# Four weight copies ahead of the semaphore clears, and block tables read sixteen at a time

## The reference

```python
# L0_ffn: 8 experts, hidden 256          L1_ffn: 16 experts, hidden 64, plus a shared expert
top_vals, top_idx = jax.lax.top_k(x @ Wg, 2)       # L1: logits + router_bias
probs = softmax(top_vals)
for e in range(E):
    u, v = x @ W1[e], x @ W2[e]
    out = out + ((silu(u) * v) @ W3[e]) * weights[..., e]
# L3_ffn: 8 experts, hidden 512
h = gelu(x @ W1[e].T + b1[e]);  y = h @ W2[e].T + b2[e];  out = out + y * w_e
```

## Time and profile before

| | us |
|---|---|
| median of 3 runs | 920.49 (919.72 to 921.42) |
| profiled execution, its own time | 919.85 |
| its span on the core | 918.1 |
| mean granted clock of PE | 0.903 of full |
| PE busy | 765.5 (83%) |
| DVE, ACT, POOL busy | 601.6, 497.4, 428.4 |

### The profile page before, as it was taken

The page is one execution under the profiler, slowest core; times in us unless marked ns, Lnnn a source line. Parts: engine busy times, 40 slices in busy tenths (PEclk is TensorE's granted clock), DMA queues, the critical chain, the costliest instruction groups (busy, mean ns, idle before and its releaser), DMA issues. The chain is left out here.

```text
span 918.1 us, 21278 instructions
## 1 busy us (share of the span) xinstructions
PE 765.5 (83%) x6415; PEld 582.6 (63%) x6415; DVE 601.6 (66%) x1816; ACT 497.4 (54%) x1344; POOL 428.4 (47%) x767
## 2 busy tenths in 40 slices
PE   3999996999679998888987876999969667659991
PEld 1565565798456776767764754666649445439991
DVE  5899995244467887777855556999957727623433
ACT  1576664676246765566662651777764322226663
POOL 3246665100534556565534327666316706724541
PEclk9999997899799999999999997899999875569996
DMA  7999940342100000000001541100000330112215
GB/s 258 382 403 404 296 166 28 78 95 68 24 7 14 13 14 25 13 26 14 14 19 54 126 121 30 25 19 24 4 1 2 96 112 32 47 51 62 72 52 153
DMA packets 69279, 78.97 MB, mean 86 GB/s; under 512 B 12848, under 2 KB 58560, under 8 KB 68912
## 3 DMA queue, kind: packets, MB, share of 16 engines
q1 hardware_dynamic: 55760, 60.64, 20.5%
q0 software_dynamic: 6368, 13.38, 5.0%
q10 hardware_dynamic: 7040, 3.58, 1.4%
HBM read 31.61 MB, written 45.96 MB: 84 GB/s over the span
## 5 line engine op out<-in xcount | busy, mean ns | idle before, releaser
L1398 PE MATMUL banks<-exps,work 128*128 128x128 f32 x718 | 106.2, 284 | 15.5 <-ACT exps L1458 10.4
L330 POOL DMA_INDIRECT routed_region<-routed_lines,line_slots x96 | 96.0, 1000 | 29.4 <-issue 25.3
L1398 PEld LDWEIGHTS banks<-exps,work 128*128 128x128 f32 x718 | 91.3, 194 | 22.2 <-ACT exps L1458 16.1
L774 ACT ACTIVATE probs_keymajor<-banks 128x512 f32<-128x512 f32 x128 | 69.9, 595 | 37.3 <-PE banks L584 37.3
L265 POOL TENSOR_TENSOR small<-small,half_and_eps 128x1 f32<-128x1 f32 x144 | 82.6, 573 | 11.3
L550 PE MATMUL banks<-work 32*128 32x512 f32 x256 | 78.8, 693 | 4.2 <-DVE exps L667 3.2
L658 DVE TENSOR_REDUCE small<-banks 128x8 f32<-128x1024 f32 x64 | 77.5, 1211 | 4.9 <-PE banks L557 3.7
L667 DVE TENSOR_TENSOR exps<-banks,small 128x1024 f32<-128x1024 f32 x64 | 77.7, 1215 | 0.4
L362 POOL DMA_INDIRECT late_results<-routed_region,line_slots x64 | 63.3, 990 | 24.8 <-issue 23.8
L584 PE MATMUL banks<-consts,exps 128*128 128x128 f32 x512 | 72.8, 288 | 1.1 <-ACT work L805 1.1
L584 PEld LDWEIGHTS banks<-consts,exps 128*128 128x128 f32 x512 | 59.4, 149 | 18.6 <-issue 12.3
(11 more groups left out here) (274 smaller groups left out, 1834.4 us busy)
## 6 DMA issues: line engine op xcount, KB each, us to landing
routed_region<-mid SPq DMA_DIRECT2D x52, 528.0 KB, 5.5
exps<-routed_region SPq DMA_DIRECT2D x125, 66.0 KB, 2.0
weights_f<-in_weights_f SPq DMA_DIRECT2D x1, 4096.0 KB, 17.7
routed_region<-work SPq DMA_DIRECT2D x63, 64.0 KB, 1.8
weights_f<-in_weights_f SPq DMA_DIRECT2D x3, 1024.0 KB, 10.7
shifted_rows<-work SPq DMA_DIRECT2D x16, 128.0 KB, 1.8
work<-expert_results SPq DMA_DIRECT2D x8, 256.0 KB, 4.6
routed_region<-routed_lines,line_slots POOLq DMA_INDIRECT x96
```

Of the source, the lines that this page charges most:

```text
L330: nc.gpsimd.indirect_dma_start(k.regions[layer % 2], bass.IndirectOffsetOnAxis(k.slots[:, b, j:j + 1], 0), k.line[:, b % LINES, j, :], Non ...
L774: nc.scalar.activation(k.pT[:, g * 512:(g + 1) * 512], bank[:, PT + g % 2, :], ACT.Copy).then_inc(s.pT, 1)
L1398: last = nc.tensor.matmul(bank[:, 2 + m % 4, i * T:(i + 1) * T], tile.weights[:, m % COPIES, i * 128:(i + 1) * 128], tile.gotT[:, m % 2, : ...
```

## The change

Two edits. A constant `READ = 16` takes the place of 8 in all reads of the tables: SP, PE, the copying engine and ACT now read at blocks 0, 16 and 32 only, sixteen words, sixteen, and the last seven (39 blocks) or fifteen (47). ACT's reads of odd rows have eight words, eight and seven. And in the second layer POOL, after its waits for the sent lines and the row table, reads its offsets and makes the copies of blocks 0 to 3, and only then waits for `sg` 4 and clears the semaphores; the copies from block 4 on follow. What is computed, and every other instruction, is the same.

```diff
--- before.py
+++ after.py
@@ -1260,6 +1260,7 @@
                                                              skip_runtime_bounds_check_because=why)
         return values
 
+    READ = 16
     TOTALS, ENDS, TABLE = 1, 2, 3
     OVER, NEED, COEF, PAST, LINES_AT, OFFS, OWN = range(1, 8)
     SHARE_GAP, SHARE_ALL = 2, 6
@@ -1273,14 +1274,13 @@
         if biased:
             sp.dma_start(tile.b2[:, :], a.b2_3[0:n, :].rearrange("e d -> (e d)").partition_broadcast(128)).then_inc(s.b2, 16)
         sp.wait_ge(s.steps, LINES_AT)
-        rows_ = list(registers(mybir.EngineType.SP, row_i[:, 0:8], REGIONS[layer % 2] * SHARE - T))
+        rows_ = list(registers(mybir.EngineType.SP, row_i[:, 0:READ], REGIONS[layer % 2] * SHARE - T))
         for slot in range(LINES):
             sp.wait_ge(ld.sent[slot], lines_sent(layer + 1, slot))
 
         def load(m):
-            if m > 0 and m % 8 == 0:
-                c8 = min(8, nb - m)
-                rows_.extend(registers(mybir.EngineType.SP, row_i[:, m:m + c8], REGIONS[layer % 2] * SHARE - T))
+            if m > 0 and m % READ == 0:
+                rows_.extend(registers(mybir.EngineType.SP, row_i[:, m:min(m + READ, nb)], REGIONS[layer % 2] * SHARE - T))
             if m >= RING:
                 sp.wait_ge(s.xT, m - RING + 1)
                 if not linear:
@@ -1387,9 +1387,8 @@
             nc.tensor.transpose(bank[:, m % 2, 0:T], tile.got[:, m % RING, 0:D], k.c["ident"]).then_inc(s.xT, 1)
 
         def up(m):
-            if m % 8 == 0:
-                c8 = min(8, nb - m)
-                offs.extend(registers(mybir.EngineType.PE, off_up[:, m:m + c8], (n - 1) * up_step))
+            if m % READ == 0:
+                offs.extend(registers(mybir.EngineType.PE, off_up[:, m:min(m + READ, nb)], (n - 1) * up_step))
             pe.wait_ge(s.xT_out, m + 1)
             pe.wait_ge(s.copied, m + 1)
             if m >= 4:
@@ -1432,9 +1431,8 @@
 
         def step(m):
             if m == len(offs):
-                c8 = min(8, nb - m)
                 table, top = (off_up, (n - 1) * up_step) if unit == 1 else (off_own, (n - 1) * PER)
-                offs.extend(registers(kind, table[:, m:m + c8], top))
+                offs.extend(registers(kind, table[:, m:min(m + READ, nb)], top))
             if m >= COPIES:
                 engine.wait_ge(s.up, m - COPIES + 1)
             copy(tile.weights[:, m % COPIES, 0:wide], ups[:, bass.ds(offs[m] * unit, wide)]).then_inc(s.copied, 1)
@@ -1474,9 +1472,8 @@
             act.wait_ge(s.up, m + 1)
             if m >= hidden_ring:
                 act.wait_ge(s.y, m - hidden_ring + 1)
-            if m % 8 == 0:
-                c8 = min(8, nb - m)
-                offs.extend(registers(mybir.EngineType.Activation, off_own[:, m:m + c8], (n - 1) * PER))
+            if m % READ == 0:
+                offs.extend(registers(mybir.EngineType.Activation, off_own[:, m:min(m + READ, nb)], (n - 1) * PER))
             for i in range(chunks):
                 last = nc.scalar.activation(tile.hidT[:, m % 3, i * T:(i + 1) * T], bank[:, 2 + m % 4, i * T:(i + 1) * T],
                                             ACT.Gelu, bias=k.cols["b1"][:, bass.ds(offs[m] + i, 1)])
@@ -1495,7 +1492,7 @@
 
         def store_odd(m):
             if m // 2 == len(odd_rows):
-                odd_rows.extend(registers(mybir.EngineType.Activation, row_i[:, m:min(m + 8, nb):2],
+                odd_rows.extend(registers(mybir.EngineType.Activation, row_i[:, m:min(m + READ, nb):2],
                                           REGIONS[layer % 2] * SHARE - T))
             store(act, m, odd_rows[m // 2])
 
@@ -1648,13 +1645,17 @@
             for slot in range(LINES):
                 pool.wait_ge(ld.sent[slot], lines_sent(layer + 1, slot))
             pool.wait_ge(s.steps, LINES_AT)
+        if narrow:
+            copied = copy_weights(pool, mybir.EngineType.Pool, nc.gpsimd.tensor_copy, [], 1)
+            pool.wait_ge(s.steps, OFFS)
+            for m in range(COPIES):
+                copied(m)
+        if linear:
             if shared:
                 pool.wait_ge(s.sg, 4)
             sems.clear_own(pool)
         if narrow:
-            copied = copy_weights(pool, mybir.EngineType.Pool, nc.gpsimd.tensor_copy, [], 1)
-            pool.wait_ge(s.steps, OFFS)
-            for m in range(nb):
+            for m in range(COPIES, nb):
                 copied(m)
         for m in range(0 if linear else nb):
             pool.wait_ge(s.to, m + 1)
```

## The result

| | before | changed |
|---|---|---|
| median of all runs | 920.80 (10 runs, 915.76 to 923.79) | 928.61 (10 runs, 923.26 to 933.47) |
| ratio | | 1.0078, 95% interval 1.0053 to 1.0103 |
| profiled execution, span | 919.85, 918.1 | 933.47, 931.3 |

The kernel got slower by 7.2 us by the ratio, where +2.1 was forecast and 925.0 was the upper end. The sign was right; the size was wrong, and the result lies outside the range. The profiled execution of the changed kernel is the slowest of its ten, so the spans overstate the loss: a table by stretches shows where the 13.2 us between them lie. Starts are those of SP's first table read and of PE's `up` products in the timelines; `up` is L1397 now.

What follows compares the result with a forecast made beforehand. PE was taken to bound the first and third layers, and the second apart from its late start and exposed reads. 1.35 - 3.85 + 4.6 = +2.1 us on the profiled 919.85, then 0.64 to the median: 922.6, range 919.0 to 925.0.

Steps and rivals of the forecast that it cites:

- What a read costs: Table reads, all layers: sixteen words cost double eight, 3.55 us on ACT and 3.97 on DVE in the third, 1.15 elsewhere.
- The rival of a flat aligned read: Table reads: aligned sixteen words cost hardly more than eight, under 0.7 us on PE, giving 920.1 us; chance 18%.
- that of one price per read: Table reads: every read costs the same whatever its length, -8.9 us in all, giving 911.6; chance 4%.
- Starts: From each layer's table read to its first `up`: +0.6, -2.15 and +1.55 us in first, second and third layer.
- Just covered, nothing: Second layer: the fifth copy, now behind the clears, ends at 504.9, before `up(4)` is due at 505.2; no cost.
- the rival with 6%: Second layer: the clears make the fifth copy miss `up(4)`, the start's gain shrinks by a microsecond, 923.6 us; chance 6%.
- Sum +1.35: First layer: PE's longer first read adds 0.6 us and the reads at blocks 16 and 32 add 0.75.
- Clock. -1.0: Second layer: without the idleness at the start PE keeps 2.4 GHz throughout, -1.0 us, bounds 0 and 1.7.
- Reads. -0.7: Second layer: fewer, longer reads on ACT and PE and less crowding behind ACT's save 0.7 us.
- forecast -3.85: Second layer in all: start -2.15, clock -1.0 and reads -0.7 us.
- I take its 1.2 us as covered: Third layer, block 16: PE's own read hides behind a block's queued matmuls, no cost, bounds 0 and 0.6 us.
- one rival, in the third layer: Third layer: the clock falls after PE's idleness at the start and block 16, costing 1.7 us, 924.3; chance 20%.

Runs made afterwards that it cites:

- e4: The changed kernel with the offset table's halves 48 words apart instead of 47: 918.4 us, ratio 0.9961 to the kernel before.
- h3: The changed kernel with the offset table's halves 50 words apart: 918.3 us in its one run, beside 902.5 for the kernel before on that chip.
- e1: The changed kernel with reads of eight again, so the moved copies alone: 919.2 us, ratio 0.9978 to the kernel before.
- h4: The changed kernel with reads of eight, table halves 48 words apart and ACT's odd rows read contiguously, on another chip: 893.4 us, ratio 0.9902 to the kernel before.
- h1: The changed kernel with PE reading its third-layer offsets two blocks ahead, on another chip: 903.7 us in its one run, beside 902.5 for the kernel before.
- g2: The changed kernel with PE's first table read of each layer ahead of the first transposes: 925.25 us, ratio 1.0057 to the kernel before.
- e3: The changed kernel with reads of eight in the third layer alone: 923.35 us, ratio 1.0021 to the kernel before.
- g1: The changed kernel with PE reading its third-layer offsets two blocks before it needs them: 930.0 us, ratio 1.0124 to the kernel before.
- e2: The changed kernel without the move, so clears before all copies and reads of sixteen kept: 934.0 us, ratio 1.0141 to the kernel before.

## Why the prediction was right in sign and wrong in size

- **What a read costs: right.** Word by word for DVE and ACT in the third layer and for the strided reads, double for the rest. The reason for the first kind was left as "the second half"; e4 and h3 show that it is where the half begins: from byte 192 of the tile the words are cheap, from 188 or 200 they are not. That cheap words are fetched in wide pieces is an inference from this and from seven words costing more than eight. The rival of a flat aligned read (18%) and that of one price per read (4%) both fell, by PE's 1.12 us.
- **Starts: right.** +0.5, -2.2, +1.5 against +0.6, -2.15, +1.55. In the third layer there is some luck in it: PE waited 2.12 us for DVE's copy, as forecast, but from run to run this start also depends on when the first blocks arrive by DMA (5.96 in e1 and 7.30 in h4, both with reads of eight words).
- **The fifth copy, "Just covered, nothing": nearly.** The copy ended within 0.3 us of the forecast, but `up(4)` came 0.45 us late, since the first four blocks need 0.62 us each where 0.69 was reckoned. The clears bind from case to case, by up to 1.0 (h1, `up(4)` 1.61 behind `up(3)`): the rival with 6% came true in part.
- **First layer, "Sum +1.35": wrong, measured +2.5.** The reads were right: the intervals of blocks 15 and 16, 1.65 and 1.82, add about 0.65 where 0.75 was forecast. The term that is missing is the clock: I priced the longer first read as idleness alone, and half a microsecond more of idleness was followed by 0.57 in 175 to 179, another 1.3 us. I had reckoned with a fall only where PE already stood still for over 2 us.
- **Second layer, "Clock. -1.0": wrong, measured about 0.** I took away the cause of one fall and did not ask what else empties PE. In e1 the fall moved to block 31; in the changed kernel it came behind the doubled ACT read at block 7. Seven profiles have these reads in the second layer (g2 with PE's first one earlier) and show the size: 39.9 and 40.6 us in g2 and h3, without a fall, 41.2 to 41.9 in e3, e4, the changed kernel and h1 with one, 43.1 in g1 with two. So a fall costs about 1 us, as priced, but the change exchanged one for another. The long read makes the fall likely there, not certain: g2 and h3 have the same long block 7 (2.5 us) and none.
- **Second layer, "Reads. -0.7": wrong, about +0.2.** g2 has no fall and its fifth copy in time, and its `up`s took 39.9, only 0.9 less than before, where clock and reads together were to give -1.7. The fall of the kernel before had cost 1.1 (blocks 3 to 5 took 3.14 us, 2.04 in g2), so fewer and longer reads gained nothing. With the clock, the reads and the fifth copy, of the forecast -3.85 the layer gave -1.5.
- **Third layer, "I take its 1.2 us as covered": wrong, measured +0.8 of the layer's +5.8 against +4.6.** Each cover was judged with the other waits absent. PE's read is hidden while its sequencer runs ahead of queued matmuls; DVE's long read, which I had put two lines above, stops exactly that. g1, h1 and e4 show it. The gap ahead was sized right (0.66), the block in all came 1.74 us later where 0.7 was forecast.
- **The range** held the forecast's terms as independent errors and gave the clock one rival, in the third layer; that fall, behind block 16, did not come (1.00 from 860 to 900 us). The three misses are 1.1 + 2.3 + 1.2 = 4.6 us of the 5.1 that separate forecast and ratio.

## What to carry to other kernels

Before reading more words at once, see from the trace what a word costs and where the table begins: here one word of padding for each half was worth ten microseconds to the long reads; with short contiguous reads and the moved copies it made a kernel 1% faster than the one before. A longer read saves nothing if its price grows with its words; it only gathers small covered stalls into large bare ones. And judge each cover with the other new waits in place: a sequencer that waits has no lead left to hide a read in, and PE, whose clock mostly lasted through small gaps, may lose it behind one large one (five of the seven second layers above).

## What the runs showed of the hardware

- A table read of 8 or 16 neighbouring words that begins 0 or 192 bytes into its tile, or a multiple of 32 behind that, took 0.55 and 1.02 us on ACT, 0.61 and 1.22 on DVE. From byte 188 they took 1.77 and 3.45 on ACT, 1.98 and 3.85 on DVE, 0.22 and 0.25 us a word; sixteen from byte 200 took 3.47 and 3.89. An offset that is a multiple of 8 is not enough; whether 16 is, or 32 is needed, was not tried. Seven words took 0.97 and 1.18, more than eight. The Trainium skill ("Runtime: NRT & Kernel Launch", section Instruction fetch mechanics) gives about 200 ns a register even in bulk: the reads from 188 and 200 agree, those from 192, 0.07 us a word, do not.
- The granted clock fell behind 1.1 us of idleness right ahead of the first layer's products (seven of eight profiles; in the changed kernel PE was also busy only 0.75 of the 2 us from 172 to 174), but the place varies from run to run: the second layer, with the same long reads, had one fall, none (g2, h3) or two (g1).
- Runs of one kernel on one chip lay up to 13 us apart (e2, 927.8 to 941.2), more than the change is worth, and 5.3 of the 13.2 us between the two profiles lay ahead of the code that was changed.
